# Four row blocks instead of four column blocks: how an LSTM step's partial sums lie in PSUM

## The reference

```
x = x + rnn(x)     # h_t = tanh(x_t Wx + b + h_{t-1} Wh),            Wh 512x512
x = x + ssm(x)     # 4-tap convolution, softplus/tanh, linear scan, 64 states
x = x + lstm(x)    # A_t = x_t Wx + b + h_{t-1} Wh,                  Wh 512x2048
                   # i,f,o = sigmoid(A[0:512]),(..),(..); g = tanh(A[1536:2048])
                   # c_t = f*c_{t-1} + i*g ;  h_t = o*tanh(c_t)
x = x + lowrank(x) # x (base + A_n B_n^T), one matrix per sequence
```

## Time and profile before

| | us |
|---|---|
| median of 3 runs | 4421.66 (4418.98 to 4426.92) |
| the profiled execution | 4419.02 |
| its span, first to last instruction | 4417.1 |
| PE busy, matmuls / weight loads | 3655.3 / 2960.4 |
| VectorE busy | 3634.3 |
| ScalarE / GpSimd busy | 1559.4 / 1291.6 |
| mean granted TensorE clock | 0.983 of full speed |

### The profile page before, as it was taken

The page is one execution under the profiler, slowest core; times in us unless marked ns, Lnnn a source line. Parts: engine busy times, 40 slices in busy tenths (PEclk is TensorE's granted clock), DMA queues, the critical chain, the costliest instruction groups (busy, mean ns, idle before and its releaser), DMA issues.

```text
span 4417.1 us, 252254 instructions
## 1 busy us (share of the span) xinstructions
PE 3655.3 (83%) x106672; PEld 2960.4 (67%) x106672; DVE 3634.3 (82%) x20882; ACT 1559.4 (35%) x6724; POOL 1291.6 (29%) x4519
## 2 busy tenths in 40 slices
PE   7888888888888888888888888888888888888775
PEld 4566667676667676666676666777666767666653
DVE  5588888888888888888888888888888888888766
ACT  4233333333333333333333333333333333333321
POOL 0223332233332223333233333232333222333311
PEclk9899999999999999999999999999999999999999
DMA  7100000000000000000000000000000000000000
GB/s 247 42 4 9 9 6 8 8 6 8 8 6 8 8 6 8 8 8 6 8 9 6 8 8 6 9 8 6 8 8 6 9 8 6 8 6 4 6 5 7
DMA packets 18979, 62.51 MB, mean 14 GB/s; under 512 B 3942, under 2 KB 4510, under 8 KB 14834
## 3 DMA queue, kind: packets, MB, share of 16 engines
q1 hardware_dynamic: 17612, 46.54, 3.3%
q10 hardware_dynamic: 294, 0.33, 0.0%
HBM read 38.34 MB, written 8.39 MB: 11 GB/s over the span
## 4 chain that ended last, share of the span: by engine, by line
DVE 40%; PE 33%; ACT 11%; POOL 8%; issue 7%; SPq 1%; DMA 1%; DVEq 0%; ACTq 0%; POOLq 0%
PE ps_lstm L968 30%; DVE lstm_sums L754 11%; DVE lstm_arg L760 7%; DVE lstm_h_scaled L783 4%; ACT lstm_gates_2c L521 4%; ACT lstm_tanh_c L526 3%; DVE lstm_gates_2c L771 3%; POOL stage L371 3%; DVE lstm_ig_fc L766 2%; DVE lstm_h_parts L791 2%; POOL stage L372 2%; DVE rnn_h_parts L857 2%; DVE lstm_h_parts L787 2%; DVE lstm_o_scaled L775 2%; DVE rnn_arg L821 2%
## 5 line engine op out<-in xcount | busy, mean ns | idle before, releaser
L968 PE MATMUL ps_lstm<-lstm_Wh_parts,lstm_h_parts 128*20 128x256 f16 x65472 | 2027.8, 276 | 638.1 <-DVE lstm_h_parts L791 633.2
L968 PEld LDWEIGHTS ps_lstm<-lstm_Wh_parts,lstm_h_parts 128*20 128x20 f16 x65472 | 1508.0, 92 | 1146.6 <-DVE lstm_h_parts L791 945.3
L521 ACT ACTIVATE lstm_gates_2c<-lstm_arg 128x32 f32<-128x32 f32 x2048 | 469.8, 229 | 1624.7 <-DVE lstm_arg L760 1623.8
L754 DVE STREAM_TRANSPOSE lstm_sums<-ps_lstm 128x256 f32<-128x256 f32 x2048 | 912.1, 445 | 137.1 <-PE ps_lstm L968 86.9
L344 POOL COPY lstm_sums<-lstm_in 128x32 f32<-128x32 f32 x2048 | 417.8, 213 | 1368.2 <-DVE lstm_arg L760 1354.5
L1007 PE MATMUL ps_rnn<-rnn_Wh_parts,rnn_h_parts 128*20 128x128 f16 x32736 | 646.7, 221 | 46.2 <-DVE rnn_h_parts L859 46.1
L760 DVE TENSOR_REDUCE lstm_arg<-lstm_sums 128x32 f32<-128x96 f32 x2048 | 536.0, 262 | 120.9 <-DVE lstm_sums L754 19.6
L1007 PEld LDWEIGHTS ps_rnn<-rnn_Wh_parts,rnn_h_parts 128*20 128x20 f16 x32736 | 550.9, 93 | 99.1 <-DVE rnn_h_parts L859 82.7
L526 ACT ACTIVATE lstm_tanh_c<-lstm_gates_2c 128x8 f32<-128x8 f32 x2048 | 413.2, 202 | 394.3 <-DVE lstm_gates_2c L771 384.4
L546 ACT ACTIVATE rnn_h<-rnn_arg 128x16 f32<-128x16 f32 x1024 | 221.2, 216 | 771.0 <-DVE rnn_arg L821 771.0
L857 DVE TENSOR_SCALAR rnn_h_parts<-rnn_h 128x16 f16<-128x16 f32 x1024 | 240.0, 234 | 292.1 <-ACT rnn_h L546 292.1
(11 more groups left out here) (176 smaller groups left out, 3390.3 us busy)
## 6 DMA issues: line engine op xcount, KB each, us to landing
layer_plus_2I<-in_L_cond_w SPq DMA_DIRECT2D x16, 1024.0 KB, 6.1
out<-out_rows SPq DMA_DIRECT2D x128, 64.0 KB, 1.9
x_rows<-in_x SPq DMA_DIRECT2D x31, 256.0 KB
lstm_Wx<-in_L_cond_Wh SPq DMA_DIRECT2D x1, 4096.0 KB, 19.2
lstm_Wx<-in_L_cond_Wx SPq DMA_DIRECT2D x1, 4096.0 KB, 14.2
layer_plus_2I<-in_L_cond_Wh SPq DMA_DIRECT2D x1, 1024.0 KB, 9.3
rnn_Wx<-in_L_cond_Wx SPq DMA_DIRECT2D x1, 1024.0 KB, 11.3
lstm_in<-in_L_cond_w SPq DMA_DIRECT2D x1, 1024.0 KB, 9.1
```

The source lines that it names most:

```text
L521: A.activation(gate[h][:, 0:G, :].rearrange("p g q -> p (g q)"), arg[h][:, :, :].rearrange("p g n -> p (g n)"), ACT.Tanh, scale=gate_scale ...
L754: return mark(V.transpose(tr[h][s % 2][:, :, 0:QC], psL[h][:, 0:HW].rearrange("p (g c) -> p g c", c=QC)))
L968: ins = mm(psL[h][QC * j:QC * j + LO + NB, 0:HW], hls[:, k, :], whl[:, k, h, e, j, :], start=(k == 0 and e == 0), stop=(k == KB - 1 and e ...
```

## The change

`psL[h]` is now filled in four row blocks r of 64 columns. Block r holds the gate columns 64 r to 64 r + 63 of the 256; its sums go to rows 4 r + n (hi) and 16 + 4 r + n (lo) of each group of 32 rows, in the same 64 PSUM columns as those of the other blocks. To get there, `hls` is padded with zeros to 44 columns, h's parts lie at columns 12 to 15 and 28 to 31, and the stationary operand of block r is the 32-column slice that starts at 12 - 4 r: it has h in the rows of block r and zeros in those of the others, so that all blocks can accumulate into one place. `whl` is laid out by block (`gate_part`), the transpose reads 64 columns, GpSimd's copy and VectorE's reduce write and read the same numbers of elements as before in the new order.

```diff
+LB = 4
+LQ = LB // HB
+LI = G // LQ
+LW = HW // LB
+LN = NB * LB
+LZ = LN - NB
+LM = LO + LN
...
-        hls = sb("lstm_h_parts", [P, KB, LO + NB], F16)
+        hls = sb("lstm_h_parts", [P, KB, LZ + LM], F16)
...
-        tr = [[sb(f"lstm_sums_{h}{e}", [P, HG, XS + NB]) for e in range(2)] for h in range(NH)]
+        tr = [[sb(f"lstm_sums_{h}{e}", [P, HG // LB, 3 * LO]) for e in range(2)] for h in range(NH)]
...
+        def gate_part(v, g):
+            return v.rearrange("p j (q b i c) -> p j q b i c", q=LQ, b=HB, i=LI)[:, :, g % LQ, :, g // LQ, :]
...
-                        Q.tensor_copy(tr[h][s % 2][:, :, XS:XS + NB],
-                                      xl[par][:, s, h * HG:(h + 1) * HG, :]).then_inc(S[f"lstm_in_ready{h}"], 1)
+                        Q.tensor_copy(tr[h][s % 2][:, :, XS:XS + LN],
+                                      xl[par][:, s, h * HG:(h + 1) * HG, :].rearrange("p (i r) n -> p i (r n)", r=LB)).then_inc(S[f"lstm_in_ready{h}"], 1)
...
-                        A.activation(whl[:, k, h, 0, :, g * HB * QC:(g + 1) * HB * QC].rearrange("p j (b c) -> p j b c", b=HB),
+                        A.activation(gate_part(whl[:, k, h, 0, :, :], g),
...
-                    return mark(V.transpose(tr[h][s % 2][:, :, 0:QC], psL[h][:, 0:HW].rearrange("p (g c) -> p g c", c=QC)))
+                    return mark(V.transpose(tr[h][s % 2][:, :, 0:QC], psL[h][:, 0:LW].rearrange("p (i c) -> p i c", c=QC)))
...
-                    three = tr[h][s % 2][:, :, :].rearrange("p g (s n) -> p g s n", n=NB)[:, :, 0:XS // NB + 1:LO // NB, :]
-                    V.tensor_reduce(arg[h][:, :, :], three.rearrange("p g s n -> p g n s"), AX.X, ALU.add
+                    three = tr[h][s % 2][:, :, :].rearrange("p i (s m) -> p i s m", m=LO)[:, :, :, 0:LN]
+                    V.tensor_reduce(arg[h][:, :, :].rearrange("p (i r) n -> p i (r n)", r=LB), three.rearrange("p i s m -> p i m s"), AX.X, ALU.add
...
-                    return mark(V.tensor_tensor(half(hls, h)[:, :, 0:NB], o3, t3, ALU.mult))
+                    return mark(V.tensor_tensor(half(hls, h)[:, :, LZ:LZ + NB], o3, t3, ALU.mult))
...
-                    V.tensor_tensor(half(hls, h)[:, :, LO:LO + NB], half(hl, h)[:, :, s, :], half(hls, h)[:, :, 0:NB], ALU.subtract
+                    V.tensor_tensor(half(hls, h)[:, :, LZ + LO:LZ + LO + NB], half(hl, h)[:, :, s, :], half(hls, h)[:, :, LZ:LZ + NB], ALU.subtract
...
                     for h in range(NH):
-                        for j in range(NQ):
-                            last = mm(psL[h][QC * j:QC * j + LO + NB, 0:HW], cond_l[:, k, :], w5[:, h, j],
-                                      start=(k == 0), stop=(k == KB - 1), tile_position=(0, QC * j))
+                        for r in range(LB):
+                            for j in range(NQ):
+                                last = mm(psL[h][QC * j:QC * j + LM, 0:LW], cond_l[:, k, LZ - NB * r:LZ - NB * r + LM],
+                                          w6[:, h, j, r // HB, r % HB], start=(k == 0 and r == 0),
+                                          stop=(k == KB - 1 and r == LB - 1), tile_position=(0, QC * j))
...
-                                for j in range(NQ):
-                                    ins = mm(psL[h][QC * j:QC * j + LO + NB, 0:HW], hls[:, k, :], whl[:, k, h, e, j, :],
-                                             start=(k == 0 and e == 0), stop=(k == KB - 1 and e == 1), tile_position=(0, QC * j))
+                                for r in range(LB):
+                                    for j in range(NQ):
+                                        ins = mm(psL[h][QC * j:QC * j + LM, 0:LW], hls[:, k, LZ - NB * r:LZ - NB * r + LM],
+                                                 whl[:, k, h, e, j, LW * r:LW * (r + 1)], start=(k == 0 and e == 0 and r == 0),
+                                                 stop=(k == KB - 1 and e == 1 and r == LB - 1), tile_position=(0, QC * j))
```

More of the change, by code:

```diff
@@ L131, in resid_stack_kernel @@
         cond_r = sb("cond_rnn_scaled", [P, KB, LO + NB])
-        cond_l = sb("cond_lstm_scaled", [P, KB, LO + NB])
+        cond_l = sb("cond_lstm_scaled", [P, KB, LZ + LM])
         b_rsc = sb("b_rnn_scaled", [P, KB])
@@ L663, in _ @@
             V.tensor_scalar(b_rsc[:, :], b_rnn, xscale_r[:, :], None, ALU.mult).then_inc(r_scaled, 1)
-            prep(V.tensor_scalar(cond_l[:, :, 0:NB], condT, 2 * H_SCALE, None, ALU.mult), wait=False)
+            prep(V.tensor_scalar(cond_l[:, :, LZ:LZ + NB], condT, 2 * H_SCALE, None, ALU.mult), wait=False)
             vec.wait_ge(ln_std, 1)
@@ L709, in prepare @@
                     s4 = whl32[:, k, g * D:(g + 1) * D].rearrange("p (h b j c) -> p h j b c", h=NH, b=HB, j=NQ)
-                    hi0, lo0, hi1, lo1 = [whl[:, k, h, e, :, g * HB * QC:(g + 1) * HB * QC].rearrange("p j (b c) -> p j b c", b=HB)
+                    hi0, lo0, hi1, lo1 = [gate_part(whl[:, k, h, e, :, :], g)
                                           for h in range(NH) for e in range(2)]
@@ L939, in prepare @@
                     pe.wait_ge(l_src, G * (k + 1))
-                    w5 = whl32[:, k, :].rearrange("p (g h b j c) -> p h j g b c", g=G, h=NH, b=HB, j=NQ)
+                    w6 = whl32[:, k, :].rearrange("p (i q h b j c) -> p h j q b i c", q=LQ, h=NH, b=HB, j=NQ, c=QC)
                     for h in range(NH):
-                        for j in range(NQ):
-                            last = mm(psL[h][QC * j:QC * j + LO + NB, 0:HW], cond_l[:, k, :], w5[:, h, j],
-                                      start=(k == 0), stop=(k == KB - 1), tile_position=(0, QC * j))
+                        for r in range(LB):
[3 more added lines that the diff above has]
+                                          stop=(k == KB - 1 and r == LB - 1), tile_position=(0, QC * j))
                     last.then_inc(lstm_h0_mm, 1)
```

## The result

| | before | after |
|---|---|---|
| median, us | 4423.97 (4 runs) | 8794.98 (8793.75 to 8797.74, 4 runs) |
| ratio | | 1.988 [1.985, 1.992] |
| span of the profiled execution | 4417.1 | 8791.9 |
| mean granted TensorE clock | 0.983 | 0.774 |

A forecast was written before the change was run, and what follows sets the result against it. PE and VectorE take turns, neither full. Terms 0.19 - 0.21 + 0.92 + 0.19 - 0.20 = +0.89 us a step, x 1023 = +910, +5 for L943: 5337 us by the median, range 4750 to 6300.

The forecast's parts named there:

- e: Instruction fetch for PE's bursts: PE starves at block borders, +0.92 us a step in the LSTM and +0.19 in the RNN.
- F: Time from asking for a block of 256 PE instructions to having it: 1.9 us taken, 0.9 lower bound, 2.6 upper end.
- My own check: PE instructions a step: 2.3 blocks x 1.9 us = 4.4 us at least, below the forecast step of 5.0.
- a: Pace of PE's array in LSTM bursts: 64 quads of 0.031 us take 1.96 us where 16 took 1.77, +0.19 a step.
- b: VectorE's transpose out of PSUM, 192 columns shorter: -0.21 us a step on the path, through transpose(1).
- c: PE's loads of 32 columns for 20: 0 to +0.05 us, taken as 0.
- d: L943, four times the instructions beside other work in chunk 0: 0 to +15 us once, taken as 5.
- f: Other layers' irregular work: two thirds of its 0.30 us a step lies beside VectorE's longer wait for PE, -0.20.
- the signs that I named: Profile signs: L968 x261,888, L754 near 240 ns, idle ahead of it about 900 us, 0.9 us gaps, 2370 packets, clock 0.98.
- Rival 1: PE's instruction fetch stays hidden, several blocks ahead or one back within 0.98 us: 4320 us (4230 to 4415), chance 0.12.
- Rival 2: On PE, pairs, not columns, set the pace: +1.6 us a step, 6050 us, or worse; chance 0.12, two thirds for 6050.
- a case of 8400 us and a figure near 9000: On PE, four groups' loads following one another, +4.1 us a step, 8400; the skill's 25 ns for every matmul, near 9000.

The follow-up runs named there:

- e4: The kernel before with only the first 64 of 256 columns transposed for each half, PE unchanged: 4280 us, ratio 0.9665.
- e1: The changed kernel with two row blocks of 128 columns instead of four of 64: 5164 us, ratio 1.167.
- e2: The changed kernel with the products of the lo parts of the weights left out: 5162 us, ratio 1.167.
- e3: The kernel before with 192 straight-line pairs of 16 columns a step added behind the RNN's matmuls: 9335 us.
- e9: The kernel before with 192 added pairs a step, run as a PE hardware loop of 4 rounds of 48: 6411 us.
- e8: The kernel before with 32 added pairs a step, run as a PE hardware loop of 8 rounds of 4: 7578 us.
- e5: The kernel before with 192 added pairs a step, run as a PE hardware loop of 8 rounds of 24: 8616 us.

## Why the prediction was wrong

**The step that failed is e, in its F.** I took a block to cost F = 1.9 us, from the back edge to the packet's end in the earlier trace rows. That the next block is asked for only when PE enters one was right, and so was the packet's delay and length (1.15 and 1.2 us here, 0.9 to 1.05 and 0.9 there). What I left out is the time from the packet's end to the first instruction out of it, 1.4 us. The earlier trace rows couldn't show it, as PE wasn't waiting there, and I took "landed" for "usable". What passes in the 1.15 us before the packet and in the 1.4 us behind it, no row shows. The round trip is 3.77 us here, and 3.5 to 4.0 in most places where a single block lies between two restarts.

**The error doesn't stay a term, it changes the regime.** With F = 1.9, a pause between bursts was long enough to have one block in hand, and I counted one starved border a step. With 3.7 even the pauses are too short, so nearly every block costs F. Put into my sum as it stands, F = 3.7 gives 0.19 - 0.21 + 2.72 + 0.64 - 0.20 = +3.14 us a step, some 7640 us; the rest up to 8795 is mostly borders that I had counted as covered. My own check, blocks a step x F, was then no longer a lower bound but the answer: 592 / 256 x 3.7 = 8.6 us; measured, first to last start of L765, 209.8 to 8777.5 over 1023, 8.38:

```profile
L765 DVE STREAM_TRANSPOSE lstm_sums<-ps_lstm x2048: 242/250/253, 209.8 to 8777.5; 128x64 f32<-128x64 f32 x187
```

I gave 2.6 us as F's upper end, the worst that I had seen, though neither edge showed when the block could be used. The earlier trace rows did hold a bound: one round of the loop takes 263 us for 52 blocks, 5.1 us each, so F isn't more than that on average, and nothing that I had read put it lower. That should have been the upper end, and 592 / 256 x 5.1 = 11.8 us a step the top of the range.

**The other terms.** a: a quad of 64 columns was to take 0.031 us; in the burst of 128 it takes (1.22 - 0.198) / 31 = 0.033. Right, and without weight. b: 250 ns for a forecast of about 240; in a kernel that isn't starved (e4) worth 0.144 us a step, not 0.207. Why less isn't shown; on e4's page the chain lies for 17% on ScalarE, where it was 11%. c wasn't measured by itself; the 0.033 us of a quad with loads of 32 columns leaves little for it. d: the line that was L943 is busy for 4.3 us, so nothing. f can't be read off by itself: the chain now lies almost wholly on PE and its waits, and the other layers' matmuls are in it. Of the signs that I named, the number of L982's matmuls (261,888) and of packets (2372 for near 2370) came true; the wait ahead of the transposes was to be of the order of 900 us and is 4423, the gaps about 0.9 us and are 1.76 and 2.54 in the rows above. PE's clock, which I expected at 0.98, fell to 0.774. These rows show it (us, busy by engine, granted clock third from the right), for the pause and the burst after it:

```profile
4005.60:4008.10 2.50, 0.00 (x0) 0.00 (x0) 0.51 (x2) 0.23 (x1) 1.26 (x3) 0.81 0.00 0
4008.13:4009.70 1.57, 1.57 (x120) 1.57 (x124) 0.00 (x0) 0.00 (x0) 0.00 (x0) 0.50 0.03 10
```

The burst at clock 0.50 (1.2 GHz) takes 1.83 us for 121 matmuls where the one at full clock took 1.22 for 128, and still the next block begins 3.77 us after each of them began: where the work of a block, slow clock and all, stays under the fetch, the slow clock costs nothing. e1 and e2, 0.97 and 0.86 with the same time, agree. Where the block's work is longer it does cost, as in e3.

**The rivals.** Rival 1 (fetch hidden) was decided by F against 0.98 us; F is nearly four times that. The passage of the Trainium skill that I weighed for it ("Runtime: NRT & Kernel Launch", "Instruction fetch mechanics") gives PE's buffer eight blocks; no run here behaves as if more than one were ahead: in the rows from 4011.90 on, one block of about 4 us of work lets PE run one block on without a pause, and then it stops. Rival 2 had a case of 8400 us and a figure near 9000, a price for each of the 256 matmuls, both near the result for a wrong reason: by the number alone they would look confirmed. The burst of 128 in 1.22 us, 0.033 us for a quad and under 10 ns for a matmul, and e9 rule both out.

## What to carry to other kernels

Count instructions, not only busy time: divide a stretch's PE instructions (two for each matmul) by 256 and multiply by 3.8 us; if that comes near the stretch's time, splitting matmuls costs more than anything it shortens elsewhere, and merging them may pay. In the profile this shows as idle "issue" with nothing named, ahead of whatever instruction a block happens to begin with, runs of 128 matmuls or a multiple of it, and span over packets of the instruction queue near 3.8 us. A latency read where nobody waited for it is a lower bound: take the rate at which the kernel before uses the resource as the upper one.

## What the runs showed of the hardware beyond this

A jump back in a small loop on PE costs about 0.4 us though its target needs no fetch (e8: 0.41 us a round with 4 pairs; from the first round to the second it was less, 0.26), so a loop pays for itself only with many pairs a round: straight-line pairs cost 3.8 us / 128 = 30 ns each when starved, looped ones 0.4 us a round and 6.6 ns each.

The granted clock fell without long pauses: in e8, whose rounds of four 16-column matmuls stand 0.22 us apart, it was 0.835 on average, in e5 with 24 a round 0.874, in e9 with 48 a round and pauses of 0.19 us 0.988. What makes the difference was not tried.
